# Another place, another wait and another number of the memsets between GpSimd's scatters

## The reference

```python
x = x + layernorm(linear_attention(layernorm(x)))      # 16 heads of 8, a running sum over each sequence
x = x + layernorm(moe(layernorm(x)))                   # below

shared = new_gelu(xf @ Wfc_s + bfc_s) @ Wproj_s + bproj_s        # 128 -> 512 -> 128
probs = softmax(xf @ Wr);  topk_p, topk_i = top_k(probs, 2)      # 8 experts, 2 of them for each token
topk_p = topk_p / sum(topk_p)
routed = sum over e of (new_gelu(xf @ Wfc[e] + bfc[e]) @ Wproj[e] + bproj[e]) * gate[:, e]
moe = shared + routed
```

## Time and profile before

| | |
|---|---|
| median of 3 executions | 385.08 us (383.65 to 385.88) |
| the profiled execution | 383.65 us, of which its span 381.9 us |
| busy share PE, PEld, DVE, ACT, POOL | 88%, 76%, 75%, 67%, 74% |
| memsets of `spare` | 36, from 204.7 to 324.0 us |
| blocks' scatters on POOL | from 222.6 to 368.4 us |
| TensorE clock granted, mean | 0.968 |

### The profile page before, as it was taken

One profiled execution on the slowest core, in us unless ns is written; L12 is line 12 of the kernel. 1 busy time (PEld: TensorE's weight loads), 2 busy tenths in 40 slices (PEclk: granted clock), 3 DMA queues, 4 the chain that ended last, 5 costly groups with the idle time before them and its releaser, 6 DMA issues.

```text
span 381.9 us, 8153 instructions
## 1 busy us (share of the span) xinstructions
PE 335.8 (88%) x2497; PEld 291.8 (76%) x2497; DVE 285.6 (75%) x687; ACT 256.3 (67%) x692; POOL 282.1 (74%) x371
## 2 busy tenths in 40 slices
PE   7878787998998998989898968589999999989891
PEld 3537485896886868868597858489999999979871
DVE  4999897799998999899944435365555459687667
ACT  4959864887986987768255845246555677688664
POOL 8878798578788787888767877877666777766640
PEclk9989996999999999999999998889999999999998
DMA  6577767575472516143088347769888879988426
GB/s 197 163 208 200 153 175 118 117 206 142 141 198 71 173 41 183 40 138 100 30 255 264 105 125 170 212 187 272 252 254 261 250 242 381 335 244 260 125 62 195
DMA packets 53522, 69.18 MB, mean 181 GB/s; under 512 B 6365, under 2 KB 37386, under 8 KB 53482
## 3 DMA queue, kind: packets, MB, share of 16 engines
q1 hardware_dynamic: 47556, 58.58, 54.7%
q0 software_dynamic: 4544, 9.35, 7.2%
q10 hardware_dynamic: 1382, 0.79, 0.8%
HBM read 40.06 MB, written 18.15 MB: 152 GB/s over the span
## 4 chain that ended last, share of the span: by engine, by line
PE 28%; DVE 16%; ACT 12%; another core or an unknown queue 9%; issue 8%; POOL 3%; ACTq 0%; DVEq 0%
PE bS L1550 6%; PE bO L1550 5%; PE bO L1334 4%; DVE KV L1701 3%; ACT hs L1153 3%; DVE KV L1692 3%; ACT hs L1024 2%; PE bV L1523 2%; PE bV L1525 2%; PE bV L1524 2%; POOL expert_lists L707 1%; DVE X L1624 1%; PE bT L1378 1%; ACT w_hi L1133 1%
## 5 line engine op out<-in xcount | busy, mean ns | idle before, releaser
L830 POOL DMA_INDIRECT expert_results<-yb,yrow x78 | 78.6, 1007 | 37.3 <-issue 25.7
L707 POOL DMA_INDIRECT expert_lists<-rows,pos x64 | 63.9, 998 | 23.0 <-issue 18.3
L1701 DVE TENSOR_TENSOR_SCAN KV<-bS,KV 128x1024 f32<-128x1024 bf16 x32 | 72.8, 2277 | 0.7 <-POOL KV L733 0.4
L1334 PEld LDWEIGHTS bO<-wout_rot,Z 128*128 128x128 f32 x512 | 60.3, 192 | 9.3 <-POOL Z L789 4.9
L1334 PE MATMUL bO<-wout_rot,Z 128*128 128x128 f32 x512 | 63.0, 277 | 3.6 <-POOL Z L742 1.7
L2146 DVE COPY yrow<-xb 128x2 int32<-128x2 int32 x24 | 7.7, 320 | 41.7 <-PE bS L1550 15.8
L1153 ACT ACTIVATE hs<-bV,KV 128x256 f32<-128x256 f32 x56 | 21.9, 476 | 20.7 <-remote 7.5
L1550 PE MATMUL bO<-KV,hs 128*128 128x128 f32 x232 | 31.2, 288 | 3.9 <-ACT hs L1153 3.5
L1550 PEld LDWEIGHTS bO<-KV,hs 128*128 128x128 f32 x232 | 29.0, 201 | 5.2 <-ACT hs L1153 4.6
L1304 PE MATMUL bA<-w2s_sb,hs 128*128 128x128 f32 x224 | 28.9, 278 | 0.0
L1304 PEld LDWEIGHTS bA<-w2s_sb,hs 128*128 128x128 f32 x224 | 27.3, 193 | 0.2
(11 more groups left out here) (369 smaller groups left out, 991.9 us busy)
## 6 DMA issues: line engine op xcount, KB each, us to landing
KV<-packed_weights SPq DMA_DIRECT2D x21, 578.0 KB
Z<-packed_weights SPq DMA_DIRECT2D x18, 578.0 KB
xb<-expert_lists SPq DMA_DIRECT2D x39, 129.0 KB
vr<-vr SPq DMA_DIRECT2D x16, 224.0 KB, 2.5
shared<-expert_results SPq DMA_DIRECT2D x7, 512.0 KB
vr<-vr SPq DMA_DIRECT2D x16, 192.0 KB
vr<-vr SPq DMA_DIRECT2D x16, 160.0 KB
vr<-vr SPq DMA_DIRECT2D x16, 128.0 KB
```

Source lines behind the costliest of these rows:

```text
L707: g.indirect_dma_start(out=lists, out_offset=bass.IndirectOffsetOnAxis(ap=pos[:, m:m + 1], axis=0), in_=rows[:, m // TILES, m % TILES, :], ...
L830: g.indirect_dma_start(out=results, out_offset=bass.IndirectOffsetOnAxis(ap=yrow[n][:, c], axis=0), in_=yb[n][:, c, :], in_offset=None).th ...
L1334: ins = t.matmul(bO[:, j * D:(j + 1) * D], Z[:, d, j * P:(j + 1) * P], wout_rot[:, d], start=False, stop=True, skip_group_check=True)
L1701: v.tensor_tensor_scan(w, ps_keep, w, 0.0, ALU.mult, ALU.add).then_inc(s["kv_sum"], 1)
```

## The change

Three things are altered, all on POOL. The number of blocks that have a memset goes from 27 to 12. In these blocks the memset stands after both scatters of the block and no longer between them. And POOL waits for a memset right after it has issued it; before, it waited for it only ahead of the next memset. The last also holds for the nine memsets among the list scatters. In all there are 21 memsets where there were 36.

```diff
             AT_END = 4
-            PAIRED = 27
+            PAIRED = 2 * NBUF
...
             def still():
 
-                if stills[0]:
-                    pool.wait_ge(s["stilled"], stills[0])
                 stills[0] += 1
                 g.memset(spare[:], 0.0).then_inc(s["stilled"], 1)
+                pool.wait_ge(s["stilled"], stills[0])
...
                         in_=yb[n][:, c, :], in_offset=None).then_inc(blk_scat[n], 16)
-                    if b < PAIRED and c == 0:
-                        still()
+                if b < PAIRED:
+                    still()
```

## The result

The changed kernel takes 386.94 us (median of 20 executions, 385.47 to 389.41), the kernel before 384.55 us beside it (20 executions): the ratio is 1.0063, 95% interval 1.0041 to 1.0086, or 2.4 us slower. The forecast was 388.0 us and 3.0 us slower, with a range of 379.5 to 392.0. The profiled execution took 386.62 us, with a span of 384.7 us (before: 383.65 and 381.9).

What follows compares the result with a forecast made beforehand. PE was taken to set the steady pace, POOL nearly nowhere the bound, though unbroken scatters delay others. 0 (dense) + 3.0 (catching up) + 0 (steady) = +3.0 us on 385.1, rounded 388.0 us; range 379.5 to 392.0.

Steps and rivals of the forecast that it cites:

- (a): Each memset on POOL: waiting right behind it costs the next scatter 0 to 0.61 us, taken as 0.61.
- (b): Memset behind the pair: a backlogged block costs 3.43 us instead of 2.82, leaving POOL 3.7 us behind at block 12.
- (c) The catching up: From block 12 on, POOL's scatters run without a pause and hold up the others: 3.0 us, bounds 0.6 and 4.5.
- (c) The steady blocks without a memset: Blocks 12 to 26 in the steady state: the lost memsets only lengthen the pause to 1.2 us, cost 0.
- the working idea of the prediction: While scatters follow one another without a pause, other engines' waits end late, some 0.7 us after the run.
- (d): Dense stretch, 205 to 250 us: longer pauses could regain lost PE time, 0 to about 8 us; taken as 0.
- The list of waiters in (b): Who waits for POOL's late work: DVE, for the scatter six blocks ago, and SP, for the lists at block 13; neither near.
- Rival 2: Faster: longer pauses end the late releases of 205 to 250 us and catching up costs little; 380.1 us, chance 0.22.
- Rival 3: Much slower: dense stretch waits lengthen by 4.6 us and catching up costs 4.5 us; 394 us, chance 0.08.

Runs made afterwards that it cites:

- T alone: Kernel before with one edit, the memset between a block's scatters only for the first 12 blocks instead of 27: 388.39 us, ratio 1.0086.
- the mixture: Kernel before with waited memsets among the list scatters and behind the pairs of blocks 0 to 5, the old order from block 6 on: 384.18 us, ratio 0.9976.
- W alone: Kernel before with one edit, POOL waits for each memset right behind it, memset still between the scatters for 27 blocks: 381.87 us, ratio 0.9925.
- P: The edit that puts the memset behind a block's two scatters; alone on the kernel before, for 27 blocks: 395.22 us, ratio 1.0148.

## Why the prediction was right, and where it was not

**The place and the mechanism were right.** Scatters at 0.30 us without a pause begin at block 12, for 9.8 us (forecast 7 to 10), and ScalarE and VectorE stand on an unknown release with an idle TensorE. Their waits of 8.03 and 7.19 us are longer than the forecast 3 to 5. The changed kernel is 2.4 us slower by the medians where 3.0 was forecast. But the total is the sum of larger terms of both signs that the prediction had mis-sized, and that they come out near its 3.0 us is in good part luck.

**(a) The waited memset, 0.61 us: right ahead of a block, wrong within a row of scatters.** The memset and its next scatter, among the lists and ahead of a block:

```profile
214.90 0.43 POOL L690 MEMSET spare<- 128x384 f32 x1
215.61 0.96 POOL L706 DMA_INDIRECT expert_lists<-rows,pos  x1 [0.28 <-POOL spare L690]
...
224.96 0.44 POOL L690 MEMSET spare<- 128x384 f32 x1
226.22 0.97 POOL L829 DMA_INDIRECT expert_results<-yb,yrow  x1 [0.82 <-POOL spare L690]
```

The wait costs 0.28 - 0.17 = 0.11 us where it is the only thing between, and 0.65 us where the wait for `blk_yr` and the increment behind it stand too. The prediction had taken its 0.61 from the earlier trace rows, a scatter that has the wait for `blk_yr` and that increment ahead of it, and laid it on the list scatters as well. The Trainium skill (Advanced Engine Details and Errata, Network/Comms) gives 50 to 100 ns for reading a semaphore; the 0.11 us is close to that, the 0.65 us is not.

**(b) The lag at block 12, 3.7 us: half.** A block does cost 3.48 us (forecast 3.43), but a pair of list scatters 2.93 and not 3.43 us, so that block 12's first scatter starts at 277.19 us and not at 279.0; before, it was 275.29.

**(c) The catching up, 3.0 us: 7.2 us.** The bounds of 0.6 and 4.5 us didn't hold it: TensorE lost 64 matmuls here. Two things are missing in the term. The waits were scaled from runs of four (2.4 to 2.7 us) to 4.5 us at most and came to 7 and 8 us for a run of eight. And the clock was left out: 4.1 us are idle time, inside the bounds, and 3.1 us are what TensorE lost at the lower clock behind it. The 11.1 us that the prediction counts as lost in the dense stretch of before lack this part too: 257 matmuls are the work of 28.9 us at 8.9 per us, so that 16.1 of the 45 us were lost.

**(c) The steady blocks without a memset, 0: 2.6 us.** This step failed. T alone shows the same with no lag at all, for +0.9%. The mean pause behind a block is near the forecast 1.2 us (1.3 from 300 to 326 us), but the pauses aren't equal. Every fourth block, two pairs come 0.5 to 0.6 us apart, which makes a run of four, and a late release ends just behind it:

```profile
307.92 0.96 POOL L829 DMA_INDIRECT expert_results<-yb,yrow  x1 [1.85 <-DVE yb L2153]
309.18 0.95 POOL L829 DMA_INDIRECT expert_results<-yb,yrow  x1 [0.30 <-issue]
310.67 0.96 POOL L829 DMA_INDIRECT expert_results<-yb,yrow  x1 [0.53 <-issue]
311.93 0.95 POOL L829 DMA_INDIRECT expert_results<-yb,yrow  x1 [0.30 <-issue]
...
313.65 1.57 ACT L1152 ACTIVATE hs<-bV,KV 128x256 f32<-128x256 f32 x4 [3.57 <-remote]
```

The second such place is at 323.14 to 328.55 us, with 3.24 us. So the working idea of the prediction holds, for runs that are only nearly without a pause too. What failed is the step from a mean pause to "no run". It rested on one place, the pairs at 337.00 and 338.56 us of before, 0.61 us apart and without a late release. The pairs at 324.52 and 326.09 us here are 0.61 us apart as well and have one, so that pause is no safe one.

**(d) The dense stretch, 0: a gain of 6.2 us.** 4.0 us of it come from 205 to 250 us and 2.1 from 250 to 277 us. It lies inside the bounds of 0 to 8. The reason given for taking 0, that a gain there only puts TensorE ahead of GpSimd and is given back in the catching up, is what the mixture shows (80 matmuls gained, 82 lost by 297 us). So the terms (c) and (d) belong together: 7.2 - 6.2 = 1.0 us where 3.0 was forecast, and the 2.6 us of the steady blocks bring the sum to 3.6, of which the tail gives back 1.0.

**The list of waiters in (b) lacked one.** It named VectorE six blocks on and SP's wait for the lists. It left out SP's wait for the scatters of the first 21 blocks, ahead of the loads of block 27, which costs 9.5 to 10.1 us where TensorE is far enough ahead and GpSimd never catches up. In the changed kernel TensorE is later and SP waits 3.1 us, about as in before (3.4), so the forecast didn't suffer.

**The rivals.** Rival 2 (faster) has its mechanism in part: the dense stretch does gain, and W alone, the kernel with that gain and without T and P, is 0.75% faster. In the changed kernel the catching up and the blocks without a memset took more than it gave. Rival 3's first half, a longer wait in the dense stretch, didn't happen.

**What stays open.** Scatters close together go with late releases in every traced kernel on three of the four chips and in none on the third; so the spacing is a condition and not the whole cause. What on those chips shares a path with the scatters, no run here tells. Nor is it told apart whether it is the chip itself or something beside it in that session, since each chip had one. Whether the changed kernel is slower than before on the chip without late releases wasn't tried either.

## What to carry to other kernels

When spacing instructions out keeps other engines from being held up, count the smallest pause that it leaves (not the mean), and the pace, which has to stay clearly under that of the engine that bounds the stage, or a lag never goes away and comes out at the next load that waits for it. A gain ahead of a backlog isn't a gain until the backlog is worked off, so read it from the stretch behind it. Price a wait from a row with the same instructions ahead of it, and repeat a difference of one per cent on another chip before trusting it.

## What the runs showed of the hardware that was not expected

- The kernel before takes 367.2 us on one chip and 384.6 to 389.8 us on the others (one session each). On the fast one none of three traced kernels has a late release; on the others every traced kernel has, of up to 12.18 us.
- During a long run of scatters at 0.30 us even TensorE has holes of 0.8 to 0.9 us inside one series of matmuls for which the profile shows no wait, while the DMA engines are busy 0.15 of the time; then it works some 7 us at the lower clock (granted 0.50 to 0.55 from 287 to 294 us).
- A scatter right behind a waited memset can take 1.44 us and not 0.96, block after block, and so keep GpSimd at exactly TensorE's pace.
- A waited memset of 0.12 us between pairs of scatters, with 0.82 us of idle time behind it, kept the blocks free of late releases; an unwaited one of 0.44 us, with 0.17 us behind it, on another chip, did not.
